# Cross attention with its scores made once: VectorE subtracts the maxima, the probabilities are turned on TensorE

## The reference, cut to what matters

```python
    def _L0_xattn_ref(query, key, value, Wq, Wk, Wv, Wo):
        ...
        scores = jnp.einsum('bhqd,bhkd->bhqk', Q, K) / jnp.sqrt(jnp.float32(D_K))
        causal = jnp.where(jnp.tril(jnp.ones((S, S), dtype=bool)), 0.0, NEG_INF).astype(scores.dtype)
        scores = scores + causal[None, None, :, :]
        attn = jax.nn.softmax(scores, axis=-1)
        heads = jnp.einsum('bhqk,bhkd->bhqd', attn, V)
        ...
    x = x + _L0_attn_ref(_layernorm(x, axis=-1), ...)
    x = x + _L0_xattn_ref(_layernorm(x, axis=-1), ctx_1024, ctx_1024, ...)
    x = x + _L0_ffn_ref(_layernorm(x, axis=-1), ...)
```

## Time and profile before

| | |
|---|---|
| median of 3 runs | 1214.93 us (1214.87 to 1220.33) |
| profiled execution | 1225.85 us |
| span of its trace | 1224.1 us |
| PE busy | 1034.5 us, 85% |
| DVE busy | 687.6 us, 56% |
| ACT busy | 496.5 us, 41% |
| POOL busy | 120.3 us, 10% |
| mean granted clock of PE | 0.914 |

### The profile page before, as it was taken

The page is one execution under the profiler, slowest core; times in us unless marked ns, Lnnn a source line. Parts: engine busy times, 40 slices in busy tenths (PEclk is TensorE's granted clock), DMA queues, the critical chain, the costliest instruction groups (busy, mean ns, idle before and its releaser), DMA issues.

```text
span 1224.1 us, 26890 instructions
## 1 busy us (share of the span) xinstructions
PE 1034.5 (85%) x11548; PEld 852.1 (70%) x11629; DVE 687.6 (56%) x1985; ACT 496.5 (41%) x836; POOL 120.3 (10%) x125
## 2 busy tenths in 40 slices
PE   6767988989799887989789887988889897997687
PEld 5653877678676676768676776867776686766576
DVE  2554167662686447672676437782676527861564
ACT  4341344424534354433534354434544344332232
POOL 8100010100201011000201011000201001000100
PEclk9776689978999998999999998999999998996789
DMA  6100001000100001000100001000010000000000
GB/s 173 35 1 1 2 2 35 10 2 2 44 1 10 2 11 35 10 2 2 44 1 10 2 10 36 10 1 2 13 32 10 2 2 9 1 10 2 9 1 18
DMA packets 28409, 18.54 MB, mean 15 GB/s; under 512 B 7394, under 2 KB 26883, under 8 KB 28291
## 3 DMA queue, kind: packets, MB, share of 16 engines
q1 hardware_dynamic: 26402, 12.35, 3.8%
q0 software_dynamic: 1280, 4.20, 1.1%
q10 hardware_dynamic: 608, 0.27, 0.1%
HBM read 12.62 MB, written 4.19 MB: 14 GB/s over the span
## 4 chain that ended last, share of the span: by engine, by line
PE 61%; DVE 21%; ACT 11%; issue 4%; POOL 2%; POOLq 0%; DVEq 0%
PE banks L533 8%; PE banks L720 6%; PE banks L676 6%; PE banks L659 6%; PE banks L522 4%; PE banks L523 3%; PE banks L524 3%; ACT PXUT L997 3%; PE banks L651 3%; ACT KQ L962 3%; PE banks L771 2%; PE banks L629 2%; DVE sil L1264 2%; DVE mx L1316 2%; PE banks L490 2%
## 5 line engine op out<-in xcount | busy, mean ns | idle before, releaser
L941 ACT ACTIVATE sil<-banks,b 128x512 f32<-128x512 f32 x144 | 99.7, 693 | 213.2 <-PE banks L524 211.1
L1264 DVE SCALAR_TENSOR_TENSOR sil<-banks,b,sil 128x512 f32<-128x512 f32 x128 | 95.7, 748 | 142.0 <-ACT sil L941 125.7
L533 PE MATMUL banks<-w,hT 128*128 128x128 f32 x1152 | 158.2, 282 | 15.0 <-DVE hT L1271 8.6
L533 PEld LDWEIGHTS banks<-w,hT 128*128 128x128 f32 x1152 | 157.9, 200 | 14.3 <-DVE hT L1271 10.4
L1333 DVE RECIPROCAL rx<-banks 128x32 f32<-128x32 f32 x32 | 11.4, 358 | 237.1 <-PE banks L676 237.1
L997 ACT ACTIVATE PXUT<-banks 128x512 f32<-128x512 f32 x128 | 66.1, 602 | 154.0 <-PE banks L659 154.0
L1316 DVE TENSOR_REDUCE mx<-banks 128x8 f32<-128x512 f32 x128 | 79.4, 683 | 26.3 <-PE banks L629 26.3
L522 PE MATMUL banks<-xnT3l,w1h 128*128 128x512 f32 x144 | 75.5, 524 | 18.6 <-ACT sil L941 18.6
L1271 DVE TENSOR_TENSOR hT<-sil,banks 128x512 f32<-128x512 f32 x128 | 87.9, 687 | 4.4
L720 PE MATMUL banks<-pooled,A 128*128 128x128 f32 x512 | 77.2, 319 | 4.6 <-DVE pooled L1353 1.9
L676 PE MATMUL banks<-Vx,PXUT 128*64 128x18 f32 x2048 | 74.7, 223 | 7.4 <-ACT PXUT L997 7.4
(11 more groups left out here) (204 smaller groups left out, 1979.5 us busy)
## 6 DMA issues: line engine op xcount, KB each, us to landing
xin<-in_x SPq DMA_DIRECT2D x8, 512.0 KB, 4.5
cin<-in_ctx SPq DMA_DIRECT2D x8, 512.0 KB, 5.7
out_x<-xr POOLq DMA_DIRECT2D x16, 256.0 KB, 2.8
KQ<-in_L_attn_Wqkv SPq DMA_DIRECT2D x3, 512.0 KB, 5.5
KQ<-in_L_ffn_We SPq DMA_DIRECT2D x2, 512.0 KB, 4.4
KQ<-in_L_attn_Wo SPq DMA_DIRECT2D x1, 512.0 KB, 8.2
w<-in_L_ffn_We SPq DMA_DIRECT2D x1, 512.0 KB
KQ<-in_L_ffn_ws SPq DMA_DIRECT2D x2, 64.0 KB, 4.4
```

The lines of the kernel that those rows point to most:

```text
L533: mm(ps(e, name)[:, P * t:P * t + P], hT[:, k % 2, P * t:P * t + P], w2[:, pair[k], :], start=(n == 0 and t == 0), stop=False, skip_group_ ...
L941: nc.scalar.activation(sil[:, k % 2, :], ps(e, f"H1_{k}")[:], ACT.Silu, bias=b1[:, pair[k]:pair[k] + 1]).then_inc(sil_ready, 1)
L1264: V.scalar_tensor_tensor(sil[:, k % 2, :], ps(e, f"H3_{k}")[:], b3[:, p:p + 1], sil[:, k % 2, :], ALU.add, ALU.mult).then_inc(hid_ready, 1)
```

## The change

The scores are made a single time, with queries on the partitions (`scores`, as before). For each tile DVE takes the maxima and then subtracts them from the tile into SBUF (`shifted`, buffer `pr`, four tiles). ACT evaluates exp in place (`exp_x`). PE turns the probabilities, four 128x128 transposes for a tile (`turn_probs_x`, PSUM tiles `PT_k`), and ACT copies them to SBUF (`PT_moved`, buffer `PT`, four tiles). `values` reads these, with its column of ones as before. `turn_shifts`, `scores_T`, `split_shifts`, `shifts_moved`, `pickT`, `shiftT` and `mparts` go.

The order of the work changes too: there are six steps in place of units 12 to 17 with the block between units 16 and 17. In a step, PE turns the probabilities of the step before, makes the scores of this one, runs one unit, then turns, multiplies and projects the outputs of earlier steps. On ACT the copies, the exps and the unit's silu follow each other within a step. `norm_a` and `apply_a` of the next group, `norm_e`, `apply_e`, `pool_queries` and the moments move to later steps as the diff shows; all eight moments stand in the last one.

```diff
+        for step in range(UX + 2):
+            if 1 <= step <= UX:
+                add(g, *[f"PT_{XQ * (step - 1) + q}" for q in range(XQ)])
+            if step < UX:
+                add(g, *[f"S_{XQ * step + q}" for q in range(XQ)])
+            if step >= 2:
+                add(g, f"OT_{step - 2}")
+            if 1 <= step <= UX:
+                add(g, f"O_{step - 1}")
+            if step == UX:
                 add(n, "xnT1_0", "xnT1_1")
...
+                add(g, "xnT3_0")
+            if step > UX:
+                add(g, "gate_0")
+                add(n, *[f"M_{k}" for k in range(8)])
+            if step >= 2:
+                add(g, f"Yx_{step - 2}")
         return tiles
...
-        mx = sb("mx", [P, T, XH])
-        md = sb("md", [P, T, XH])
+        mx = sb("mx", [P, XQ, 2 * HALF // 2])
-        PT = PXUT[:].rearrange("p a b h -> p (a b h)").rearrange("p (k n) -> p k n", k=2 * XQ)
+        pr, PT = [X.rearrange("p b h -> p (b h)").rearrange("p (k n) -> p k n", k=XQ) for X in (PX, UT)]
...
-            step(nc.gpsimd.affine_select(out=shiftT[0:S].rearrange("p (b q) -> p b q", q=S),
...
-            step(nc.gpsimd.affine_select(out=pickT[0:S], in_=pickT[0:S], compare_op=ALU.not_equal, fill=1.0, base=0,
...
-            for k in range(3):
-                step(nc.gpsimd.affine_select(out=pickT[S:P], in_=pickT[S:P], compare_op=ALU.not_equal, fill=1.0,
...
-            def turn_shifts(g):
...
-            def scores_T(g, u):
...
+            def turn_probs_x(g, u):
+                for q in range(XQ):
+                    name = f"PT_{XQ * u + q}"
                     wait_free(pe, g, name)
+                    pe.wait_ge(pr_ready, XS * g + XQ * u + q + 1)
+                    for t in range(2):
+                        for j in range(2):
+                            src = pr[:, q, 256 * t + P * j:256 * t + P * j + P]
+                            c0 = 256 * j + P * t
+                            last = turn_over(ps(g, name)[:, c0:c0 + P], src, ident[:])
+                    last.then_inc(fulled(g, name), 1)
...
             def values(g, u):
...
+                pe.wait_ge(pT_ready, XS * g + XQ * u + XQ)
...
-                                      PT[:, XQ * (u % 2) + j // 2, c0:c0 + S], Vx[:, 4 * u + k, j, :],
+                                      PT[:, j // 2, c0:c0 + S], Vx[:, 4 * u + k, j, :],
...
             def turn_O(g, u):
...
+                pe.wait_ge(On_ready, UX * g + u + 1)
...
                     front_ctx(nxt)
                 if g is not None:
                     pe.wait_ge(Kx_ready, 2 * g + 2)
...
                     pe.wait_ge(V_ready, 4 * g + 4)
...
+                for step in range(UX + 2):
+                    if g is not None and 1 <= step <= UX:
+                        turn_probs_x(g, step - 1)
+                    if g is not None and step < UX:
+                        scores(g, step)
+                    unit(e, 12 + step)
+                    if g is None:
+                        continue
+                    if step >= 2:
+                        turn_O(g, step - 2)
+                    if 1 <= step <= UX:
+                        values(g, step - 1)
+                    if step == UX:
+                        if nxt is not None:
                             front_xn(nxt)
...
+                        turn_3(g, 0)
+                    if step > UX:
+                        gate_scores(g, 0)
+                        if nxt is not None:
+                            front_M(nxt, range(8))
+                    if step >= 2:
+                        project(g, step - 2)
                 if e is not None:
                     down_to(e, UNITS - 1)
...
             run(pe, both)
...
+            def PT_moved(g, u):
+                if u:
+                    wait_full(act, g, f"O_{u - 1}")
+                for q in range(XQ):
+                    moved(g, f"PT_{XQ * u + q}", PT[:, q, :], pT_ready)
...
             def exp_x(g, k):
...
-                wait_full(act, g, f"ST_{k}")
-                nc.scalar.activation(PT[:, k % (2 * XQ), :], ps(g, f"ST_{k}")[:], ACT.Exp).then_inc(ex_ready, 1)
+                act.wait_ge(dx_ready, XS * g + k + 1)
+                p = pr[:, k % XQ, :]
+                nc.scalar.activation(p, p, ACT.Exp).then_inc(pr_ready, 1)
...
+                for step in range(UX + 2):
+                    if g is not None and 1 <= step <= UX:
+                        PT_moved(g, step - 1)
+                    if g is not None and step < UX:
+                        exp_x(g, XQ * step)
+                        exp_x(g, XQ * step + 1)
+                    if g is not None and 2 <= step < UX:
+                        O_moved(g, step - 2)
+                    if g is not None and step < UX:
+                        exp_x(g, XQ * step + 2)
+                        exp_x(g, XQ * step + 3)
+                    silu(e, 12 + step)
+                    if g is None:
+                        continue
+                    if step >= UX:
+                        O_moved(g, step - 2)
+                    if step == UX:
+                        if nxt is not None:
+                            xn_moved(nxt)
+                        xn3_moved(g, 0)
+                    if step > UX:
+                        exp_gate(g, 0)
+                        if nxt is not None:
+                            for n in range(8):
                                 M_moved(nxt, n)
...
-            def maxima(g, u):
...
-            def split_shifts(g):
...
+            def shifted(g, u):
                 for q in range(XQ):
                     k = XQ * u + q
                     wait_full(dve, g, f"S_{k}")
+                    sv = ps(g, f"S_{k}")[:].rearrange("p (h s) -> p h s", s=S)
+                    link(V.tensor_reduce(mx[:, q], sv, AX, ALU.max))
+                    if u:
+                        wait_full(dve, g, f"PT_{k - XQ}")
+                    V.tensor_tensor(pr[:, q, :].rearrange("p (h s) -> p h s", s=S), sv,
+                                    mx[:, q].unsqueeze(2).to_broadcast([P, HALF, S]), ALU.subtract).then_inc(dx_ready, 1)
...
+                for step in range(UX + 2):
+                    if g is not None and step < UX:
+                        shifted(g, step)
+                    if g is not None and step == UX:
+                        apply_e(g, 0)
+                    hidden(e, 12 + step)
+                    if g is None:
+                        continue
+                    if step == 2 and nxt is not None:
+                        dve.wait_ge(x_loaded, 16 * nxt + 16)
+                        norm_a(xin)
+                    if step == 3 and nxt is not None:
+                        apply_a(xin, 2 * nxt + 1)
+                    if 1 <= step <= UX:
+                        normalise_O(g, step - 1)
+                    if step > UX:
+                        if nxt is not None:
                             pool_queries(nxt)
...
+                        gate_shift(g, 0)
+                    if step >= 2:
+                        add_x(g, step - 2)
+                        if step % 2 == 0:
+                            stats_e(g, step - 2)
+                        else:
+                            norm_e(g, (step - 3) // 2)
                 result(e, 1)
                 if g is not None:
                     gate_groups(g, 0)
...
                     gate_best(g, 0, 0)
             run(dve, both)
```

More of the change, by code:

```diff
@@ L59, in decoder_block @@
     PERIODS = [(None, 0)] + [(e, e + 1) for e in range(GROUPS - 1)] + [(GROUPS - 1, None)]
-    MOMENTS = [(), (0, 1, 2), (3, 4, 5), (6, 7)]
     def attention_tiles(e, g):
@@ L264, in decoder_block @@
             read |= {f"M_{n}": (M_ready, 8, n)}
-        read["mT"] = (mT_ready, 1, 0)
         for n in range(XS):
-            read |= {f"S_{n}": (mx_ready, XS, n), f"ST_{n}": (ex_ready, XS, n)}
+            read |= {f"S_{n}": (dx_ready, XS, n), f"PT_{n}": (pT_ready, XS, n)}
         for u in range(UX):
@@ L980, in M_moved @@
                       M_ready, ps(g, f"M_{n}")[:].rearrange("p (h b i) -> p h b i", b=GB, i=POOL))
-            def shifts_moved(g):
-                moved(g, "mT", shiftT[S:P, :], mT_ready, ps(g, "mT")[:].bitcast(bf16)[S:P, :])
+            def PT_moved(g, u):
[3 more added lines that the diff above has]
+                    moved(g, f"PT_{XQ * u + q}", PT[:, q, :], pT_ready)
             def O_moved(g, u):
@@ L1087, in both @@
                     ctx_moved(nxt)
-                for k in range(12, 17):
-                    silu(e, k)
-                if g is not None:
-                    shifts_moved(g)
-                    for u in range(UX):
-                        for q in range(XQ):
-                            exp_x(g, XQ * u + q)
-                        if u:
-                            O_moved(g, u - 1)
-                        if nxt is not None and u:
-                            for n in MOMENTS[u]:
-                                M_moved(nxt, n)
-                        elif nxt is not None:
```

(45 more changed lines are left out.)

84 lines of the change are left out of this document (2 added, 82 removed).

## The result

The changed kernel takes 1276.93 us (median of four runs, 1275.74 to 1278.28) against 1217.63 us (1214.87 to 1221.89) for the kernel before in the same batch: a ratio of 1.0484, 95% interval 1.0444 to 1.0524. It is slower, where the forecast put it (1278). Its profiled execution took 1277.4 us around a span of 1275.7; against the 1225.85 us of the profiled execution before that is +51.6, and the sum of the prediction, read from the rows of that execution, was +62.9. The medians differ by 59.3, since the profiled execution before lay 8 us above the median of its batch and the one after lay on its own.

A forecast was written before the change was run, and what follows sets the result against it. PE carries most of the chain's time, with DVE and ACT not near their limits. Six periods 79.5, less 5.6, 4.3 and 6.7, give +62.9 us: profiled 1288.7, median 1278, range 1225 to 1312.

The forecast's parts named there:

- step 0 to 1: Between last subtractions of steps 0 and 1: exp, table load, silu, copies, scores, pairs; 11.6 us at full clock.
- step 1 to 2: Between last subtractions of steps 1 and 2: PT waits for normalise_O's bank, behind silu and hidden; 13.0 us at full clock.
- step 2 to 3: Like the transition before it, plus norm_a ahead of normalise_O (2.6) and add_x (0.4); 16.0 us at full clock.
- tail: Stage after step 3's last subtraction: silu to values, closing work, turned inputs, all eight moments (7.8); 29.1 us at full clock.
- the loop: Four-bank PSUM ring: new scores need a copied PT tile's bank, copies stand behind silu; stage 77.5 us at full clock, against 68.7.
- The 6.0 us: Per stage with FFN: PE at the 1.2 GHz level adds 1.4 to scores three times, 1.8 to unit 16; bounds 0 and 10.6.
- the clock holds: Rival, chance 0.16: PE's short pieces between waits keep its clock up; sum +12, 1227 us.
- more at half clock: Rival, chance 0.16: 4.6 us more in each of seven stages, 1310 us.
- PE sets the pace and the change gains: Rival, chance 0.09: DVE and ACT run ahead, each stage is worth its -7.7 us; 1149 us.
- The stage without FFN: First to second queries, no silu, load or hidden: 67.7 against 73.3 us, -5.6 (to -14 at full clock).
- Setup: Kernel start: five POOL selections go, transposes of xn start at 30.9 instead of 37.67; -6.7 us.
- The stage without a next group: Last stage: 69.7 against 72.5 us, -2.8, with the 1.5 behind it -4.3.

The follow-up runs named there:

- e1: The changed kernel with the silu of steps 0 to 3 ahead of the step's four exps on ACT: 1181.72 us, ratio 0.9712.
- e2: The changed kernel with normalise_O (steps 1 to 3) and add_x (steps 2 and 3) ahead of hidden on DVE: 1196.84 us, ratio 0.9836.
- e7: The changed kernel with exp in place of silu in units 12 to 15 of seven periods, order kept: 1228.86 us, ratio 1.0099.
- e5: The changed kernel with PE repeating transposes in its waits, results the same: 1243.18 us, ratio 1.0217.
- e8: The kernel before with only the next group's eight moments moved to the end of the stage: 1263.55 us, ratio 1.0389.
- e3: The changed kernel with silu ahead of the exps on ACT and normalise_O and add_x ahead of hidden on DVE: 1139.53 us, ratio 0.9357.
- e4: The kernel before with pickT, shiftT and mparts built on POOL after the first x addition: 1207.16 us, ratio 0.9927.

## Why the prediction was right

**Head and transitions.** From the ends of the last subtractions (686.05, 698.91, 713.46, 731.55) and the stage's start at 678.29:

| part | forecast, full clock | with the clock | measured |
|---|---|---|---|
| head | 7.8 | 7.8 | 7.8 |
| step 0 to 1 | 11.6 | 13.0 | 12.9 |
| step 1 to 2 | 13.0 | 14.4 | 14.6 |
| step 2 to 3 | 16.0 | 17.4 | 18.1 |
| tail | 29.1 | 30.9 | 30.3 |
| stage | 77.5 | 83.5 | 83.6 |

The chain is found where the forecast had it: the silu with its load and hidden stand on the loop (e1, e2 and e7 each take some of that off and gain), the pairs come in blocks of 5.4, norm_a stands ahead of normalise_O in step 2, and ACT makes twelve loads in a steady period instead of six. The 1.5 us off the rest of the period came too: 153.71 less 83.55 is 70.2, before 140.44 less 68.72 is 71.7. One sign missed: from one block of masks to the next it is 11.0, 15.3 and 18.4 us, where 10 to 16 was named, although the forecast itself has 17.4 for the last.

**The clock.** The 6.0 us were an assumption from a stage with another pattern of waits. Filling the waits gave 5.6 of them back (e5). The rival that the clock holds fell by the 0.86 and the score matmuls of 2.33. Its price of +12 us is not confirmed by e5, which leaves the first period as it was: e5's profiled execution took 15.6 us more than the one before, its median 26 more than the kernel before beside it. Of the rival of more at half clock a part came, the last transposes (eight in 1.97, against 1.06); the larger part did not, since the values take 2.05 in the steady stage.

**The tail.** The moments were charged in full, 7.8 us, because they leave waits that they had filled. e8 shows this with no other part of the change: 6.3 us a period.

**PE sets the pace and the change gains** was the right rival to keep. Its condition was named as load, silu and hidden off the loop; e3 takes these off by order alone (and norm_a and apply_a with them), and the kernel comes to 1139.53, where the rival said 1149. That its price, PE's 7.7 us a stage, is what e3 gained is not shown.

**What was mis-sized.** *The stage without FFN* was -5.6 and became -14.0 (59.3 us); the steps came to 10.6, 9.6 and 12.8 (forecast 11.0, 11.0, 13.2), the tail to 18.5 where 24.8 was charged. In it the moments took 7.4 and not 10.0: PE had its full clock again by then. That is the end of the range that the forecast gave for this stage at full clock (-14). Part of it was lost in the next period's start, where PE waits 4.33 us for xn. *Setup* was -6.7 and became -11.1, but only a little of the excess is the change's: the transposes of xn start at 29.78, not 30.9, since the turned context takes 1.09 and not 2.0. The first moments behind it take 7.41, before 10.04, and that goes with the clock of the single execution: 0.72 before, 1.00 after, and 0.81 both in e8, which has the setup of the kernel before, and in e4, which has the starts of the changed kernel. Against e8 the setup and the stretch behind it gained 7.0 us. *The stage without a next group* was -4.3, and against the same code in e8 and e4 only 0.3 to 0.7 us came.

So the sum of 62.9 was 11.3 too high for the two profiled executions, but 9 of these lie at the start and the end of the one before, where e8 has the same code 4.1 and 5.2 us shorter. For the medians it was 3.6 too high. Within that, errors cancel (too little off the stage without FFN, too much off the one without a next group), and meeting 79.5 with 79.6 is in part luck: against the periods of e4, whose code is the same there (139.80), it would be 83.5.

## What to carry to other kernels

When work moves from a phase of its own into a loop over several engines, write down for one turn of the loop what stands ahead of each release in each engine's queue; work that doesn't belong to the loop (here a silu with its table load, and hidden) must stand where its engine waits anyway. The same instructions in another order on ACT and DVE turned +4.8% into -6.4%. And before work is moved out of another engine's waits, ask what fills them afterwards: the moments were nearly free there, and with them the clock stayed higher (0.95 against 0.86 over the stage, e8). A difference between two single profiles should be held against a third that has the same code: here it took 4 to 5 us off two terms.

## What had not been expected of the hardware

- More work on PE made the kernel faster: with 140 transposes more in a stage the granted clock went from 0.86 to 0.98 there and the period from 153.7 to 148.1 us (e5). The reverse in e8: with the moments out of its waits PE ran most of the same values in 3.5 to 3.6 us instead of 2.05.
- A table switch between two activations costs 1.40 us from start to start, 0.12 more than the load itself, and nothing like the load twice (e7).
- A shorter wait can bring the clock with it: e1 was costed at 70 us by its waits and gave 95, at a clock of 0.938 instead of 0.906. The clock's share of the 25 is not separated.
- The same code ran at different clocks in different executions: the moments of the setup took 10.04 us at 0.72 in the kernel before and 9.04 at 0.81 in e8.
